# Eight value projections of half 1 taken out of the front and set between the transposes of probabilities, in a two-layer attention kernel with an order written out by hand

## What is computed

```python
x = x + _L0_xattn_ref(_layernorm(x), ctx_1024, ...)            # local attention, 16 keys per query
x = x + _L0_attn_ref(_layernorm(x), ...)                       # RWKV-like scan
x = x + _L0_ffn_ref(_layernorm(x), ...)                        # shared and routed experts, top 2 of 8
x = x + _L1_xattn_ref(_layernorm(x), ctx_1024, ctx_1024, mask_Bx1xSxS2_fk0, ...)
x = x + _L1_attn_ref(_layernorm(x), ...)                       # linear attention and FFN
x = x + _L1_ffn_ref(_layernorm(x), ...)                        # 16 experts, capacity 32
# inside _L1_xattn_ref, 16 heads of 8, for each batch 32 queries against 512 keys:
kw = k @ Wk + bk
vw = v @ Wv + bv
weights = jax.nn.softmax(scores + mask * NEG, axis=-1)
out = jnp.einsum('bhqk,bhkd->bhqd', weights, vh)
```

## Time and profile before

| | us |
|---|---|
| median of 3 runs | 233.22 |
| the three runs | 232.96, 233.22, 234.82 |
| the profiled execution | 234.76 |
| its span in the profile | 233.0 |

### The profile page before, as it was taken

One profiled execution on the slowest core, in us unless ns is written; L12 is line 12 of the kernel. 1 busy time (PEld: TensorE's weight loads), 2 busy tenths in 40 slices (PEclk: granted clock), 3 DMA queues, 4 the chain that ended last, 5 costly groups with the idle time before them and its releaser, 6 DMA issues.

```text
span 233.0 us, 5313 instructions
## 1 busy us (share of the span) xinstructions
PE 222.0 (95%) x2010; PEld 158.9 (68%) x2010; DVE 175.5 (75%) x507; ACT 132.9 (57%) x292; POOL 34.7 (15%) x55
## 2 busy tenths in 40 slices
PE   7999899999999999789899999999999989899995
PEld 6422685657786797455567766767677788798495
DVE  2476544999974699998887789999889767735672
ACT  2204462346377456889998888799987731133030
POOL 2020001032214126302040230020001031210000
PEclk9999999999999999999998999999999999999999
DMA  6999959600000000007000430000007999300001
GB/s 198 402 422 450 421 236 228 136 0 0 0 4 0 3 0 1 0 17 166 3 0 4 104 82 0 3 3 1 3 3 264 429 408 414 159 0 3 0 3 45
DMA packets 2905, 26.88 MB, mean 115 GB/s; under 512 B 448, under 2 KB 704, under 8 KB 1344
## 3 DMA queue, kind: packets, MB, share of 16 engines
q1 hardware_dynamic: 2880, 26.54, 31.5%
HBM read 26.28 MB, written 0.26 MB: 114 GB/s over the span
## 4 chain that ended last, share of the span: by engine, by line
PE 72%; DVE 10%; DMA 9%; ACT 3%; issue 2%; SPq 2%; POOL 0%; DVEq 0%
PE bank L1419 11%; DMA late_sb<-late 9%; PE bank L1435 6%; PE bank L1295 6%; PE bank L1405 5%; PE bank L1238 4%; PE bank L1234 3%; PE bank L1273 3%; DVE ctx_sb L954 2%; PE bank L1218 2%; PE bank L1378 2%; PE bank L1649 2%; PE bank L1361 2%; PE bank L1537 2%; PE bank L1640 2%
## 5 line engine op out<-in xcount | busy, mean ns | idle before, releaser
L579 ACT ACTIVATE ctx_sb<-ctx_sb,small_sb 128x512 f32<-128x512 f32 x64 | 45.9, 720 | 3.0 <-DVE small_sb L954 2.7
L954 DVE CUSTOM_DVE_ANT_0 ctx_sb<-bank,mask_sb 128x512 f32<-128x512 f32 x64 | 41.9, 679 | 2.6 <-PE bank L1419 1.8
L1419 PE MATMUL bank<-early_sb,ctx_sb 128*128 128x128 f32 x256 | 36.6, 281 | 2.3 <-DVE work_sb L965 1.4
L1419 PEld LDWEIGHTS bank<-early_sb,ctx_sb 128*128 128x128 f32 x256 | 28.3, 142 | 15.2 <-ACT ctx_sb L579 8.3
L381 POOL TENSOR_TENSOR rstd_sb<-veps_sb,minus_half_sb 128x2 f32<-128x2 f32 (+1 forms) x15 | 11.0, 733 | 129.9 <-DVE veps_sb L674 129.9
L590 ACT COPY work_sb<-bank 128x512 f32<-128x512 f32 x40 | 22.8, 579 | 8.1 <-PE bank L1419 7.7
L1405 PE MATMUL bank<-k_sb,work_sb 32*128 32x512 f32 x128 | 18.2, 638 | 1.3 <-DVE small_sb L954 1.1
L722 DVE SCALAR_TENSOR_TENSOR work_sb<-bank,early_sb,work_sb 128x512 f32<-128x512 f32 x16 | 11.8, 747 | 8.3 <-PE bank L1273 7.9
L1238 PEld LDWEIGHTS bank<-late_sb,ctx_sb 128*128 128x128 f32 x128 | 15.4, 191 | 3.4 <-issue 3.3
L1435 PE MATMUL bank<-work_sb,v_sb 128*32 128x128 f32 x512 | 17.3, 275 | 0.0
L965 DVE COPY work_sb<-bank 128x512 f32<-128x512 f32 x24 | 16.4, 682 | 0.8 <-PE bank L1419 0.8
(11 more groups left out here) (264 smaller groups left out, 398.4 us busy)
## 6 DMA issues: line engine op xcount, KB each, us to landing
k_sb<-moe_w SPq DMA_DIRECT2D x1, 4096.0 KB, 12.4
ctx_sb<-moe_w SPq DMA_DIRECT2D x1, 4096.0 KB, 17.1
ctx_sb<-ctx SPq DMA_DIRECT2D x3, 1024.0 KB, 14.7
late_sb<-late SPq DMA_DIRECT2D x1, 2966.5 KB, 21.1
mask_sb<-ctx_tok SPq DMA_DIRECT2D x1, 2048.0 KB, 13.2
v_sb<-ctx_tok SPq DMA_DIRECT2D x1, 2048.0 KB, 27.1
mask_sb<-mask SPq DMA_DIRECT2D x4, 512.0 KB, 7.8
mask_sb<-mask SPq DMA_DIRECT2D x8, 256.0 KB, 4.4
```

What stands on the lines that cost most here:

```text
L579: s.activation(sc[u % NSC], sc[u % NSC], ACT.Exp, bias=smin[:, u:u + 1], scale=-1.0, accum_out=rsum[:, u:u + 1]).then_inc(sig("p1_ready"), 1)
L954: v.tensor_tensor_reduce(sc[u % NSC], bank[SB[u % GROUPS]][:, :], mask[:, KEYS * b:KEYS * (b + 1)], MASK_BIG, 3e38, ALU.add, ALU.min, smin ...
L1419: last = nc.tensor.transpose(bank[TB[u % 2]][:, P * k:P * (k + 1)], sc[u % NSC][:, P * k:P * (k + 1)], wt("ident"))
```

## The change

- `DEFERRED = 8`: the last eight entries of `PROJ`, the value projections of batches 8 to 15, leave stream P.
- They go into stream T on TensorE, and into the copies of ScalarE and VectorE: one after transposed unit 4, 7, 10, 13, 16, 19, 22 and 25 (`AFTER`).
- Banks 3 and 4 are now given out over one list, `SHARED`: 24 projections, then units and deferred projections as they follow one another. Each item waits for the copy of the item two before it (`released`).
- V of batch b now also waits for the copy of its values.
- `TURNS` is another table on all four engines it has rows for. The counts of L1419, L1405, L1435, L1238 and L1234 are unchanged. Stream G gives 40 turns in the table instead of 39.

```diff
+        DEFERRED = 8
+        FIRST = len(PROJ) - DEFERRED
+        AFTER = [4 + 3 * n for n in range(DEFERRED)]
+        SHARED = [("proj", i) for i in range(FIRST)]
+        for u in range(2 * UNITS):
+            SHARED.append(("turn", u))
+            SHARED.extend(("proj", FIRST + n) for n in range(DEFERRED) if AFTER[n] == u)
+        PLACE = {item: n for n, item in enumerate(SHARED)}
+        def shared_bank(kind, i):
+            return bank[3 + PLACE[kind, i] % 2]
+        def released(kind, i):
+            n = PLACE[kind, i] - 2
+            return None if n < 0 else copied(SHARED[n][1]) if SHARED[n][0] == "turn" else taker(SHARED[n][1])
...
             def projections():
-                for i, (kind, b) in enumerate(PROJ):
...
+                for i in range(FIRST):
+                    projection(i)
                     yield
...
                 for u in range(2 * UNITS):
                     pe.wait_ge(sig("p1_ready"), u + 1)
-                    if u < 2:
-                        name, n = taker(len(PROJ) - 2 + u)
-                    else:
-                        name, n = copied(u - 2)
+                    name, n = released("turn", u)
                     pe.wait_ge(sig(name), n)
...
+                    for n in range(DEFERRED):
+                        if AFTER[n] == u:
+                            projection(FIRST + n)
+                            yield
...
+                    for i in range(len(PROJ)):
+                        if PROJ[i] == ("v", b):
+                            name, n = taker(i)
+                            pe.wait_ge(sig(name), n)
```

`projection(i)` is the old body of the loop, with `shared_bank` for the bank and `released` for the wait. `copies()` on ScalarE and VectorE gets the same inner loop as `turns()`. Of the table, the beginning of one engine's turns:

```diff
     "DVE": (
-        "L18 a L a L4 a L3 a4 L a L2 a4 L a4 L a2 L2 a4 L2 a3 L a L2 P a3 L a L2 a L b L2 P a5 L a2 b a3 L a5 "
+        "L24 a3 L2 a4 L a L2 a3 L a L a6 L2 a3 L a L a2 L a L a L a2 L a2 L3 a L2 a4 L a6 b a L a P a2 P a b "
```

98 lines of the change are left out of this document (56 added, 42 removed), and 29 rows, old and new, of the table TURNS.

## The result

The changed kernel takes 238.39 us by the median of four runs (236.49 to 238.61), the kernel before 234.02 in the same comparison: 1.0169 times as long, with a 95% interval of 1.0092 to 1.0247. The forecast was 232.5, with a range up to 235.6. It was wrong in size and, by its likeliest case, in sign.

The account below looks back on a forecast made before the run. TensorE and VectorE were taken to bound by stretch, ScalarE fullest from 99.6 to 125.9 us. Terms -3.8 + 2.7 + 0.4 = -0.7 turned the profiled 234.8 into 234.1, or 232.5 by the median; range 229.8 to 235.6.

Parts of the forecast that it names:

- From the third scores: Third scores to last transposes: 6.2 us of projections less 1.4 idle, 1.7 clock and 0.4 stretched pieces, 2.7 later.
- (a): Half 0's context products: seven operands now stand ahead of the wait for the late load; gain 1.1 us.
- (b): One half 0 key projection moves from waiting time to behind the context products; cost 0 to 0.86, taken 0.3 us.
- (c): 55.7 us to the second half's context products: two key projections and a copy go later; gain 1.0 us.
- (d): 65.0 to 82.2 us: TensorE bounds and has one key projection fewer; gain 0.86 us.
- (e): 82.2 us to third scores: VectorE bounds, loses four value copies and gains two key copies; gain 1.1 us.
- The loop: Behind the third scores: 6.2 us of projections, less 1.4 idle filled and 0.4 stretched pieces; new bank wait taken as 0.
- The clock: Low clock from 125.9 us taken as gone with projections among small matmuls: 1.7 us back; the skill's rule said otherwise.
- The end: Half 1's attention output and gate: stream G pieces stand ahead on TensorE; 0.4 us later, between 0 and 0.8.
- C: Units 7 to 25: TensorE pays in the loop, little idle met, low clock stays; +2.4, 235.6 by the median; chance 0.21.
- B: The loop takes the projections for nothing: -3.2, 230.0 by the median; chance 0.27.
- D: Between first and third scores TensorE idles over 3 us, clock falls there, 1.7 not returned: +1.0, 234.2; chance 0.14.

Follow-up runs that it names:

- experiment 8: Changed kernel with one key projection of half 0 back ahead of its context products: 237.31 us; the same with before's order from batch 12's scores: 237.59.
- Experiment 7: Kernel before, nothing deferred: one wait moved, 232.43 then 233.76 us; new order up to 61 us, 235.61; that with one key projection put back, 235.22.
- Experiment 5: Changed kernel with deferred projections behind units 0, 2, 4, 7, 10, 13, 16, 19, three instead of one ahead of the third scores: 242.52 us.
- thin_front: Kernel before with the eight value projections of half 1 cut to one of four matmuls each: 236.87 us, ratio 1.0151.
- experiment 6: Eight value projections of half 1 cut to one of four matmuls each: in the changed kernel 238.39 us, in the kernel before 236.87.
- experiments 1 and 3: Changed kernel with before's order throughout, 256.84 us; with before's order only up to the third scores, 243.67; with it only behind the third scores, 249.47.
- experiment 1: Changed code with every engine in the order of before, only the eight value projections and their copies moved behind units 4 to 25: 256.84 us.
- thin_loop: Changed kernel with each of the eight deferred value projections cut to one of four matmuls, copies and waits kept: 238.39 us.
- changed_again: The changed kernel run again unchanged: 236.18 us, ratio 1.0137.
- tail_of_before: Changed kernel up to the scores of batch 12, all engines in the order of before from there on: 237.66 us.
- key_back: Changed kernel with one key projection of half 0 back at its old place ahead of the context products: 237.31 us.
- loop_of_before: Changed kernel up to the third scores, then the order of before with the deferred projections at their places: 249.47 us.
- experiments 1 to 3, 5 and 6: Includes a second one: deferral in the order of before, with ScalarE and VectorE copying directly behind the transposed unit ahead of each projection: 251.75 us.

## Why the prediction was wrong, by its own steps

**The forecast line.** This is one of the two largest errors, and it needed no experiment. "From the third scores" takes 1.7 us off because the dip at 125.9 would go. "The forecast" then takes 1.5 off because the profiled execution lies that much above the median. That 1.5 was the dip: at clock 1.00 the kernel before takes 233.57, at 0.993 235.34, and the profiled execution had 0.993. It was counted twice. With it once, the same terms give 234.1, no longer faster than before.

**(a) and (b): about right, 0.8 forecast and 0.6 measured.** In the changed kernel all eight batches of products start at 26.03, and what stands behind them starts at 33.39; in the kernel before one batch starts at 25.68, the other seven at 27.56, and what stands behind at 34.02. That is 0.6 in this pair of executions. The term that was left out is the 0.88 us that TensorE waits at 26. The moved wait alone gives 0.9 at this place in one profile, and 1.2 at the end at the same clock. How close the forecast came is partly luck, as the load's landing moves this wait by 1.1 us between traces of one order. For b, experiment 8 shows 0.2, within the spread.

**(c) and (d): right in sum.** (Three key projections stand between 57.5 us and the second half's products, five from 55.7 on; that two of them go later is right.) Up to the end of the FFN's last products (82.2 before) the terms add up to 2.7; the next piece of TensorE's queue started at 78.88 instead of 82.04, 3.2 earlier. Experiment 7 shows what the prediction didn't say: with nothing deferred the same FFN products come 0.9 later than before, not earlier. The gain is there only because the deferral emptied a place for the key projections.

**(e): this step failed, 1.1 forecast, and 0.5 lost instead.** From the piece behind the FFN's last products to the third scores it took 17.57 us before (82.04 to 99.61) and takes 18.03 now (78.88 to 96.91). That VectorE bounds there was right, and so was the price of its copies: by the steps from start to start, four copies less and two more give 1.1. What failed is that everything else on VectorE was taken to stay as long as it was. It is the same instructions in both kernels, and they take about 1.5 us more. The largest part is the scan step L873, 1.03 to the next start instead of 0.34; the norm L708, L831 and L866 are longer as well, by 0.3, 0.4 and 0.15. All three of L873, L866 and L708 start while POOL is in an instruction and end 0.3 us or so behind it. In all eight traces with the new order up to there the step of L873 takes 1.10 us, starts inside POOL's 128x768 instruction and ends 0.28 us behind it; in the ten with the order of before it takes 0.40 to 0.42, and POOL is idle. The new table has moved POOL's instruction to this place. That this is the reason is the reading that fits all 18 traces, but no run moves POOL's instruction alone.

The first scores come 4.3 earlier and the third only 2.7 because three scan steps have also changed sides. Between the first and third scores there are eight of them now (4.8 us, L849 to L873) and five before (2.6, L827 to L841), against copies of 1.40 instead of 2.04 us: +2.2 - 0.6 = 1.6, and the stretch is 10.65 instead of 9.07 long. Experiment 5 and thin_front say from the other side that VectorE sets the pace there, and that TensorE's time has nearly no value.

**The loop: this step failed too, 4.4 forecast at the same clock, 5.4 measured.** As a sum of TensorE's time it reads so: 6.2 for the projections, 0.5 of idle time taken up and not 1.4, 0.3 from stretched pieces and not 0.4. Up to unit 25 the idle time fell from 1.9 to 1.0 us, by the 0.9 of the forecast's lower end; behind it 0.4 of new idle time came in, where the forecast had nothing. That the fixed places would meet few idle pieces was said and then priced too well. Unit 25 starts at 135.35 instead of 135.57, where about 1 us earlier was named as the sign. But the sum leaves a step out. It has TensorE alone pay, and experiment 6 shows that with 4.0 us of these matmuls gone only 0.7 comes back, ScalarE being busy for 26.66 of 26.92 us. The prediction noticed that ScalarE was the fullest engine here (24.72 of 26.30) and gave its four further copies no price. The new wait was taken as 0: one such wait of 0.33 (94.75) shows in the new order, and in the orders of experiments 1 and 3, which weren't made for the projections, TensorE idles 8.5 and 8.65 us over a part of the loop.

**The clock: no gain.** Between the two profiled executions the dip's time did come back, but by chance and not by the change, because the dip comes in some runs of each kernel: 5 of 10 against 27 of 62 had none. Where TensorE was thinned without a new order the dips became more or longer. The rule that the prediction weighed (the Trainium skill, "TensorE: Matmul & The Clock Gate", section "A second HAM failure mode: psum-queue depth-cycling") has frequent short idle times between groups of matmuls as the cause, and these traces agree for the holes (0.53 for 14 us in experiment 1, 0.50 for 6 us behind one in thin_loop). They don't agree for the dip of changed_again: TensorE had been busy for 16.00 of 16.00 us when its clock fell at 76. Three more traces with the new order up to there (tail_of_before, key_back, loop_of_before) show the same.

**The end: 0.4 forecast, 0.6 measured.** Idle grew by 1.0, most of it the 1.25 at 202. The forecast counted pieces of G and not VectorE's chain ahead of them.

**The rivals.** C was nearest: third scores less than 3 us earlier (2.7), little idle met in the loop, and its own sign came, third scores after 96.5 (96.91). With its +2.4 on a profile without the double count it would have been a good forecast for the 2.6 at clock 1.00, though its reason, that TensorE pays, is only a part by experiment 6. B was wrong by the reason given against it. D named the hole, and in experiments 1 to 3, 5 and 6 the clock falls in it or close by, but not in the changed kernel's profiles.

## What to carry to other kernels

Before a sum is set against a median, put the runs in order of their granted clock, and take what a dip costs either in the sum or in the step from profile to median, never in both. Work that leaves a stretch is worth what the engine that bounds there gets, work that comes to one costs what its fullest engines pay, and an idle engine in a ring of two banks isn't room: whatever waits in its queue hands its wait to the scores behind it. When an order is made anew, compare every engine's instructions between the two milestones of each term, and how long each takes: the same one can be longer beside another engine's work.

## What was not expected of the hardware

Taking 5.3 us of matmuls off TensorE made both kernels slower by the median, by 2.2 and 2.6 us, through more stretches at 1.2 GHz: none of eight runs was above 0.986, where 27 of 62 runs of before and 5 of 10 of the changed kernel were at 1.00. A dip costs 1.5 to 1.9 us in five of the six steps of the table (0.6 in the sixth, of two and three runs), and one program can have none, one or two of them. Their place moves too: the kernel with one wait moved has its dip at 123 us in one profile and at 211 in the other. In four of the eight traces with the new order up to there it came at 76 or 77 us, after 16 us or more without idle time, behind matmuls of 8 rows (in changed_again 2 groups of them, from 72.8 on):

```profile
72.83 1.99 PE L1402 MATMUL bank<-work_sb,late_sb 8*128 8x256 f32 x8
74.75 0.71 PE L1254 MATMUL bank<-following_sb,o_sb 128*128 128x128 f32 x4
75.40 0.71 PE L1410 MATMUL bank<-late_sb,work_sb 8*128 8x128 f32 x4
```

The dip of the earlier trace rows follows the same kind of matmuls of the other half (L1361 and L1369, 120.8 to 125.5). Whether the few rows bring it wasn't tried.
